# Rotary attention of one layer rewritten: two score passes, four heads at a time in row bands of the array

## The reference, cut to what matters

```
ms = mean(X*X);  Xn = X * rsqrt(ms + EPS) * rms_w
Q = (Xn @ Wq_w.T + Wq_b).reshape(b, s, H, D_K)      # 4 sequences, 512 tokens, 16 heads of 16
K = V = Q
Qr = Q*cos + rotate_half(Q)*sin;  Kr = K*cos + rotate_half(K)*sin
A = softmax(causal(Qr @ Kr.T / sqrt(D_K)))
O = (A @ V) @ Wo_w.T + Wo_b
return pre_X + O        # pre_X is the layernorm's output; x += gate * this
```

## Time and profile before

| | us |
|---|---|
| median of three runs | 6489.69 (6486.56 to 6490.51) |
| the profiled execution, its own time | 6483.94 |
| its span, first to last instruction | 6482.1 |
| mean granted TensorE clock, share of full speed | 0.925 |

### The profile page before, as it was taken

The page is one execution under the profiler, slowest core; times in us unless marked ns, Lnnn a source line. Parts: engine busy times, 40 slices in busy tenths (PEclk is TensorE's granted clock), DMA queues, the critical chain, the costliest instruction groups (busy, mean ns, idle before and its releaser), DMA issues. The chain is left out here.

```text
span 6482.1 us, 91750 instructions
## 1 busy us (share of the span) xinstructions
PE 5360.2 (83%) x30798; PEld 3975.0 (61%) x30798; DVE 3759.5 (58%) x7849; ACT 3136.4 (48%) x9493; POOL 1195.5 (18%) x1216
## 2 busy tenths in 40 slices
PE   4899989999899999999979997888867773577769
PEld 2678777778777777877765555555544442333335
DVE  3666766666666666667653234555345555666661
ACT  1566666666666666666641113444225554333321
POOL 1222222222222222222220001111000000222210
PEclk7999999999999999999989998999979886788879
DMA  1000000000000000000010001000000000000000
GB/s 37 14 21 17 17 17 17 16 19 19 18 16 17 16 17 21 17 16 17 16 44 1 1 10 57 1 1 1 16 19 1 1 1 8 17 1 0 0 20 13
DMA packets 47176, 93.40 MB, mean 14 GB/s; under 512 B 11984, under 2 KB 19184, under 8 KB 45712
## 3 DMA queue, kind: packets, MB, share of 16 engines
q1 hardware_dynamic: 46736, 88.07, 4.6%
HBM read 85.67 MB, written 2.38 MB: 14 GB/s over the span
## 5 line engine op out<-in xcount | busy, mean ns | idle before, releaser
L857 ACT ACTIVATE dh_pb<-bank 64x128 f32<-64x128 f32 x3072 | 831.3, 271 | 272.0 <-PE bank L631 238.7
L645 PE MATMUL bank<-dh_cw,dh_pb 128*128 128x128 f32 x5120 | 701.6, 281 | 112.9 <-ACT dh_pb L857 111.4
L645 PEld LDWEIGHTS bank<-dh_cw,dh_pb 128*128 128x128 f32 x5120 | 635.7, 193 | 191.0 <-ACT dh_pb L857 164.3
L995 DVE SCALAR_TENSOR_TENSOR dh_kq<-bank,dh_conv_kq,dh_kq 128x511 f32<-128x511 f32 (+2 forms) x408 | 305.3, 748 | 184.0 <-ACT dh_kq L814 172.8
L863 ACT ACTIVATE dh_cw<-bank 128x256 f32<-128x256 f32 x640 | 245.0, 385 | 254.9 <-PE bank L645 247.6
L582 PE MATMUL bank<-hT,dh_w_kq 128*128 128x512 f32 x544 | 276.3, 632 | 82.6 <-DVE dh_kq L995 75.2
L995 DVE SCALAR_TENSOR_TENSOR dh_v<-bank,dh_conv_v,dh_v 128x511 f32<-128x511 f32 (+2 forms) x384 | 284.0, 747 | 91.3 <-ACT dh_v L814 82.3
L1669 PE MATMUL bank<-moe_h_split,moe_w 128*128 x1200 | 279.5, 383 | 22.6 <-PEq L88 15.0
L1930 POOL TENSOR_TENSOR blk_att_e<-blk_att_e,blk_att_block_share 128x128 f32<-128x128 f32 (+3 forms) x256 | 185.3, 724 | 475.7 <-DVE blk_att_block_share L1903 475.7
L594 PE MATMUL bank<-dh_w_vz,hT 128*128 128x256 f32 x1024 | 245.5, 383 | 22.0 <-ACT dh_zs L825 22.0
L262 POOL TENSOR_TENSOR ln_rstd<-ln_var_eps,nhalf 128x16 f32<-128x16 f32 x8 | 23.2, 2903 | 1266.7 <-DVE ln_var_eps L252 1266.7
(11 more groups left out here) (399 smaller groups left out, 13262.3 us busy)
## 6 DMA issues: line engine op xcount, KB each, us to landing
dh_rates<-delta_rates SPq DMA_DIRECT2D x130, 256.0 KB, 3.5
dh_w_vz<-in_L_wvz SPq DMA_DIRECT2D x17, 512.0 KB, 3.3
mod_w<-in_L_wmod SPq DMA_DIRECT2D x4, 1536.0 KB, 6.4
dh_w_kq<-in_L_wkq SPq DMA_DIRECT2D x18, 256.0 KB, 2.6
dh_wo<-in_L_wo SPq DMA_DIRECT2D x16, 256.0 KB, 4.2
moe_w<-in_L_w13T SPq DMA_DIRECT2D x1, 3200.0 KB, 16.0
x_res<-in_x SPq DMA_DIRECT2D x1, 2048.0 KB, 8.2
mla_wA<-in_L_wA SPq DMA_DIRECT2D x1, 2048.0 KB, 8.5
```

The costliest lines, as they stand in the source:

```text
L645: last = pe.matmul(square(j)[:, b, :, :], pb[j][:, b, :], src[:, :, b, :], start=True, stop=True)
L857: last = act.activation(out[half, :, o, half], src[halves[o], :, half], ACT.Copy)
L995: dve.scalar_tensor_tensor(y, pj_bank(n)[:, 0:S - i], taps(n)[:, TAPS - 1 - i:TAPS - i], y, ALU.mult, ALU.add).then_inc(s["v_cs" if i < TA ...
```

## The change

`rotary_attention` now consists of one preparation over all four sequences and one attention over all of them, both written out without a loop.

- **rotary_prep** runs the steps above as a pipeline: while sequence s is transposed, squared and normalised, sequence s-1 is projected and rotated. There is one barrier at its end. The bias, the gate and the sum of the residual part into x move to GpSimd here (L2307 to L2313). The masked keys `km` are gone: SyncE moves the rotated rows by 32 DMAs (L2230) into `keys`, where a group of four heads stands in four bands of 32 partitions, 16 rows of data and then rows of ones.
- **rotary_attend** goes through 16 groups G of four heads. First pass: scores from band i to bank i (L2390), the mask (L2397), the maximum of each row (L2476), in three parts st that hold query tiles (3), (2, 0) and (1). The negated maxima are transposed (L2405) and added to the queries as a 17th row (L2484, "shift"). Second pass, one group later: scores again, but with keys on the partitions (L2417, "turned"), into a ring of three banks, so that exp (L2525) leaves the weights as the weighing wants them; GpSimd sets the masked corner of each diagonal block to zero (L2568, L2572). Transposes and copies of the weights are gone. Weighing, two groups later (L2433): each head's values are 64 wide, 32 of them ones for the sum of the weights, so sums come out beside the values. 1/sum is exp(-ln(sum)) on ScalarE (L2533, L2537), and VectorE multiplies (L2493). The projection (L2449) and the sum into x (L2501, L2505) follow for every fourth group.

The core of the new order on TensorE and ScalarE:

```diff
+                for G in range(NG + 4):
+                    new, old, older = G < NG, 1 <= G <= NG, 2 <= G <= NG + 1
+                    if old: turn_max(G - 1)
+                    if new: scores(G, 0)
+                    if old: turned_scores(G - 1, 0)
+                    if older: weigh(G - 2, (0,))
+                    if new: scores(G, 1)
+                    if old: turned_scores(G - 1, RING)
+                    if older: weigh(G - 2, (1,))
+                    if new: scores(G, 2)
+                    if old: turned_scores(G - 1, 2 * RING)
+                    if older: weigh(G - 2, (2, 3))
+                    if old: turned_scores(G - 1, 3 * RING)
+                    if G >= 3 and (G - 3) % HPG == HPG - 1: project((G - 3) // HPG)
...
+                def scores(G, st):
+                    for i in range(HPG):
+                        after(pe, maxed, nth(G, st, i) - HPG)
+                        at = 0
+                        rows = keys[32 * i:32 * i + DK2, G, :]
+                        for t in SCORE_TILES[st]:
+                            pe.matmul(bank[i][:, at:at + (t + 1) * P], rows[:, t * P:(t + 1) * P], rows[:, 0:(t + 1) * P],
+                                      start=(at == 0), stop=False, skip_group_check=True)
+                            at += (t + 1) * P
...
+                def turn_max(G):
+                    pe.wait_ge(maxed, nth(G, 2, HPG - 1))
+                    ring_free(pe, ("turn", G))
...
+                def turned_scores(G, first):
+                    pe.wait_ge(shifted, G + 1)
+                    for n in range(first, first + RING):
+                        st, i = divmod(n, HPG)
+                        u = ("exp", G, st, i)
+                        ring_free(pe, u)
+                        at = 0
+                        r = slice(32 * i, 32 * i + DK2 + 1)
+                        for j in TURNED_TILES[st]:
+                            last = pe.matmul(ring(u)[:, at:at + (NC - j) * P], keys[r, G, j * P:(j + 1) * P],
+                                             own[r, G % 2, j * P:S], start=(at == 0), stop=(j == TURNED_TILES[st][-1]),
+                                             skip_group_check=True)
...
+                def invert(G):
+                    act.wait_ge(weighed, G + 1)
+                    after(act, normed, 2 * (G - 1))
+                    for i in range(2):
+                        at = i * HALF + 32
+                        act.activation(rec[at:at + 32, G % 2, :], bank[7][at:at + 32, :], ACT.Ln).then_inc(logs, 1)
+                    for i in range(2):
+                        own_rec = rec[i * HALF + 32:(i + 1) * HALF, G % 2, :]
+                        act.wait_ge(logs, 2 * G + i + 1)
+                        act.activation(own_rec, own_rec, ACT.Exp, scale=-1.0).then_inc(inverted, 1)
+
+                for G in range(NG + 1):
+                    if G < NG:
+                        for n in range(3 * RING):
+                            exponent(G, n)
+                    if G > 0:
+                        invert(G - 1)
+                    if G < NG:
+                        for n in range(3 * RING, 4 * RING):
+                            exponent(G, n)
...
+                def normalise(G):
+                    b, g = G // HPG, G % HPG
+                    dve.wait_ge(inverted, 2 * (G + 1))
...
+                for G in range(NG + 4):
+                    new, old, older = G < NG, 1 <= G <= NG, 2 <= G <= NG + 1
+                    if old: shift(G - 1)
+                    if new: maximum(G, 0)
+                    if new: maximum(G, 1)
+                    if new: maximum(G, 2)
+                    if older: normalise(G - 2)
+                    if G >= 3 and (G - 3) % HPG == HPG - 1: add_out((G - 3) // HPG)
```

More of the change, by code:

```diff
@@ L2190, in head_values, with rotary_prep @@
     last.then_inc(done, 1)
-def rotary_attention(k):
+HPG = 4
+NG = NB * H2 // HPG
+SCORE_TILES = ((3,), (2, 0), (1,))
+TURNED_TILES = ((0,), (1, 3), (2,))
+TURNED_AT = {0: 0, 1: 512, 3: 896, 2: 1024}
+RING = 3
+def rotary_prep(k, w, keys, vtok):
     nc, d = k.nc, k.dram
     G = P // DK2
[L2197 to L2208, removed]
-        junk = ph.sb("junk", [P, D])
[L2210 to L2225, removed]
@@ L2229, in _ @@
             def _(sp):
[L2230 to L2240, removed]
+                for b in range(NB):
+                    sp.wait_ge(rotated, b + 1)
+                    for i in range(HPG):
+                        for odd in range(2):
+                            dst = keys[32 * i:32 * i + DK2, b * HPG:(b + 1) * HPG, :].rearrange("p (g o) n -> p o g n", o=2)
+                            head = HPG * odd + i
+                            sp.dma_start(dst[:, odd, :, :], kr[head * DK2:(head + 1) * DK2, b, :, :]).then_inc(spread, 16)
@@ L2241, in _ @@
+                sp.wait_ge(spread, 16 * 2 * HPG * NB)
+            @block.tensor
+            def _(pe):
+                for s in range(NB + 1):
+                    if s < NB:
+                        after(pe, tok, 2 * s)
                         for t in range(NC):
                             for kk in range(KD):
-                                last = pe.transpose(k.bank[t // 2][:, (t % 2) * D + kk * P:(t % 2) * D + (kk + 1) * P],
-                                                    ht[:, kk, t * P:(t + 1) * P], k.ident[:, :])
+                                last = pe.transpose(bank[t // 2][:, (t % 2) * D + kk * P:(t % 2) * D + (kk + 1) * P],
+                                                    k.hT[:, kk, s, t * P:(t + 1) * P], k.ident[:, :])
@@ new lines, in _ @@
+                            if t % 2:
+                                last.then_inc(vt, 1)
+            @block.scalar
+            def _(act):
+                for s in range(NB + 1):
+                    if s < NB:
+                        for i in range(2):
+                            act.wait_ge(tk, 2 * s + i + 1)
+                            after(act, xns, NC * (s - 1))
+                            after(act, biased, s - 1)
+                            act.activation(htok[:, s % 2, 2 * i:2 * i + 2, :].rearrange("p t d -> p (t d)"), bank[i][:, :],
+                                           ACT.Copy).then_inc(tok, 1)
+                        for t in range(NC):
+                            act.wait_ge(tok, 2 * s + t // 2 + 1)
+                            after(act, sq, NC * s + t)
+                            act.activation(junk[:, :], htok[:, s % 2, t, :], ACT.Square, accum_out=ss[:, 0, s, t:t + 1])\
+                                .then_inc(sq, 1)
+                    if s > 0:
+                        b = s - 1
```

312 lines of the change are left out of this document (255 added, 57 removed).

## The result

| | before | after |
|---|---|---|
| median of the runs | 6488.8 us | 6440.4 us (6431.3 to 6441.9) |
| ratio, 95% interval | 1 | 0.9923 (0.9905 to 0.9940) |
| span of the profiled execution | 6482.1 us | 6429.5 us |
| forecast | | 6360 us (6290 to 6465) |

The change makes the kernel faster, by 48 us where 129 were forecast. The sign and the range held; the size did not.

A forecast was written before the change was run, and what follows sets the result against it. TensorE was taken to bound the attention, no engine the rest. Preparation 80, fill 1 and attention 332 make 413 us instead of 542; 6483.9 - 129 = 6355, plus 5.8 for the median: 6360 us, range 6290 to 6465.

The forecast's parts named there:

- The chain of a period at full clock, 18.0 us: Attention, one group of four heads, shift to shift: maxima, scores, exps, inversion, normalising take 18.0 us; no engine bounds it.
- The sum into x: Attention: three more sums into x, each 4 x 0.69 us on VectorE, delay a shift, 8.3 us together.
- The clock: ... I add 1.0, between 0 and 3.: Attention: TensorE idles some 4 us per period, so slow work behind it adds 1.0 us, making a period 19.0.
- The attention's ends, 47 us with the sums: Beside fifteen periods: first maxima 9.7, second group 11, last weighing to normalising 11, last projection 6.5, sums 8.3 us.
- The preparation, 80 us: Preparing four sequences as one pipeline: steps of 15.6 us, start, tail and barrier make 80 us, from 68 to 92.
- The fill costs 1 us: Ahead of the stage: the fill grows from 7.4 to about 16 us beside other work and costs 1 us.
- a selection under 3.4 us: GpSimd's corner selections, eight per group: hidden by the nearest row; above 3.4 us each they'd reach the slower outcome's point.
- The rival that the bands go one after another: Attention scores: bands don't run side by side, a period takes 27.3 us, no change at 6488 us; chance 0.06.
- the slow one: Attention: TensorE at 1.2 GHz throughout, weight loads in one line, period 30 us and more, 6570 us; chance 0.08.
- the likeliest case: The forecast's own case for the attention: periods of 17 to 21 us, total 6320 to 6400 us; chance 0.58.
- the case "longer, 21 to 26": Attention: bands partly side by side or weight loads in one line, periods 21 to 26 us, 6390 to 6465; chance 0.20.
- signs of being wrong: Period over 24 or under 16 us, selection over 2.4 us, or VectorE waiting for scores over a quarter of a period.

The follow-up runs named there:

- e2: The changed kernel with five full-array f32 products of 512 columns, thrown away, added where TensorE waits at a period's end: 6364.0 us, ratio 0.9808.
- e4: The changed kernel with GpSimd's fills moved to where VectorE doesn't stream and its gating passes waiting for VectorE's: 6413.0 us, ratio 0.9887.
- e5: As e2, but the five products added to the changed kernel are of 16 rows in one band: 6437.0 us, ratio 0.9921.
- e10: Changed kernel with e4's fills, VectorE reciprocal, normalising behind next first maxima, first weighing behind second turned scores, two full products ahead of it: 6389.2 us.

## Why the prediction was half right

It was faster as forecast, and by the mechanism forecast; the size failed, above all in one term.

- *The chain of a period at full clock, 18.0 us.* Right: 18.2 in after where the clock was up (5148.57 to 5166.79), 18.24 in e2. The sum into x, forecast at 2.8 us, delays a shift by 4.2 there.
- *"The clock: ... I add 1.0, between 0 and 3."* This is the step that failed. It measured 4.7 us, after against e2. From the first shift to the end of the attention the low clock costs 68 us by the rows below, where the sum had 15: 53 of the 71 us missing in the attention. The sum looked at the idle time alone, read the clock of a busy TensorE from heads that worked with 128-row products, and took it as so for bands. In the new order full-height work is only the weighing, the masks and the turned maxima. Its upper bound of 3 stood for one slow third of a period. Against e2 the four periods cost 3.9, 6.5, 0 and 8.2 us more: the second has a slow projection too, and in the fourth the clock stayed down through two thirds.
- *The attention's ends, 47 us with the sums.* The start ran at the low clock throughout, 0.50: 15.5 us to the first shift where 9.7 were forecast, and 17.5 to the second where 11 were. Behind the last shift, 37.0 us are near the 36.5 of the sum (a period, the last weighing and the last projection), though they are 6.5 less at the full clock of e2. The rest of the 71, some 6 us net, lies in the sums into x and in a first full group that took 22.8 us in e2 too.
- *The preparation, 80 us.* 76.9. Right in size; 5 of them were VectorE held up beside GpSimd (71.7 in e4), which the sum had not seen.
- *The fill costs 1 us.* It cost 7.3. It was priced as hidden beside other engines' work; the earlier trace rows had the fill, but not that VectorE's passes beside it slow down (846 ns a pass in before too, and 1334 in after, against 412 alone in e4).
- *Bands side by side; table loads with nothing lost; a selection under 3.4 us.* All three right: 2.09 us for four bands, 1.28 a load, 0.406 a selection. The rival that the bands go one after another is out. So is the slow one, but half of it came true: the clock stayed low for about half the time, while the weight loads didn't queue (16 records of the second part's scores in 1.17 us).
- *The range.* It held, but the likeliest case (0.58 for periods of 17 to 21 us) did not; the case "longer, 21 to 26" with 0.20 did by its number, though I had tied it to bands or weight loads and not to the clock. That the time lies in the range is luck to that extent. Of the signs of being wrong, two came: single periods of over 24 us (their mean is 23.8), and VectorE's waits for scores, 28% of the attention.

The rows behind the second point (columns of the earlier trace rows), for after from the first shift to the second, on to the last and on to the end; then for e2 from the second shift to the last and on to the end:

```profile
4912.10:4929.60 17.50, 16.73 (x88) 10.08 (x88) 7.38 (x17) 5.55 (x12) 3.16 (x8) 0.50 0.00 0
4929.60:5262.40 332.80, 263.00 (x1672) 127.01 (x1672) 130.40 (x279) 146.21 (x252) 45.71 (x116) 0.75 0.00 1
5262.40:5299.40 37.00, 23.59 (x112) 11.72 (x112) 6.19 (x9) 15.44 (x24) 3.11 (x8) 0.78 0.00 0
...
4934.00:5205.70 271.70, 264.58 (x1812) 130.74 (x1812) 130.43 (x278) 146.21 (x252) 45.54 (x116) 0.98 0.00 1
5205.70:5236.20 30.50, 25.95 (x132) 13.27 (x132) 6.26 (x10) 15.44 (x24) 3.27 (x9) 1.00 0.00 1
```

332.8 - 271.7 and 37.0 - 30.5 are 68 us together. Between the first two shifts both runs take 17.5 us, for e2 has no products thrown away there.

Not settled is what the clock goes by. The runs show that 16-row products do not hold it up where 128-row ones do; no number of rows between them is tried. The products of e2 and e5 also differ in what their operands hold, which no run separates. Against that as the cause speaks, without settling it, that the kernel before had zeros in 112 of the 128 rows of its masked keys and was granted 0.97.

## What to carry to other kernels

Where a change trades full-height matmuls for row-banded ones, or leaves TensorE waiting in each period, price the next steps at both clock levels and read the clock of periods, not the busy share. A few full-array products in a wait can pay for themselves: 4.7 us a period here for 4.6 us of otherwise idle time; behind the fall of the clock they cost double (e10). Where GpSimd's long passes and fills run beside VectorE's passes over SBUF, move one of them and see: 22 us here.

## What was not expected of the hardware

- With five 16-row products in each wait TensorE is busy 97% of the time at a mean clock of 0.77 (e5); as many full-array ones give 1.00 (e2).
- A VectorE `tensor_scalar` of 128x256 takes 349 ns alone and 1945 on average beside GpSimd passes; beside a memset 1334 instead of 412.
- VectorE's reciprocal takes 3.36 us for 128x512, five times a `tensor_tensor` of that width (0.69), and is still cheaper than Ln, Exp and two table loads on ScalarE, 5.0 us.
- GpSimd's selection takes 406 ns for 128x256, less than its multiply of the same size at 616.
